# A gated attention block with mixture of experts: another order of the engines' steps in each pass over two sequences, the experts' rows cut at 352 in place of 384, and the third output tile placed on either side of the branch

## The chip, the cores and the metric

One Trainium2 chip, one core. The metric is the device time of one execution in microseconds (us), as the median of several runs. TensorE (PE) multiplies, VectorE (DVE), ScalarE (ACT) and GpSimd (POOL) work elementwise, SyncE (SP) issues most of the transfers. Each engine runs its own instruction stream in order; semaphores join the streams.

## The reference

Sixteen sequences `x` of 128 tokens and 256 features are normalized and attend to a context in a sliding window (two batches of 1024 tokens, 16 heads of 16, blocks of 128). The result, times `tanh(g_xattn)`, is added to `x`. Then a mixture of 8 experts follows, with the two best experts for each token and room for 640 rows per expert:

```
xn = layernorm(x) * gamma + beta;  probs = softmax(xn @ Wr.T);  two best experts per token
rank = place of the (token, expert) pair among its expert's; kept if rank < 640
buf[expert, rank] = xn[token]
g, u = buf @ W12.T (halves of 2048);  h = silu(g) * u;  y = h @ W3.T
x = x + tanh(g_ffn) * sum over kept pairs of prob * y[expert, rank]
```

Run through the reference, these inputs send 225, 328, 984, 337, 706, 204, 671 and 641 rows to experts 0 to 7, so that experts 0, 1, 3 and 5 have at most 337 rows and the other four fill all 640.

## The kernel before

**Attention and routing.** Eight passes (`body`, n = 0 to 7), each over two sequences in eight steps g (one per group of four heads). Every engine has its own `body`, with the order in a step written out by hand; semaphore counts hold the streams together. A group's work goes from engine to engine: PE `scores` into one of two PSUM banks, DVE `largest` (L941), ACT `exps` (L631), two steps later PE `prob_columns` (transposes, L1317), ACT `high_probs` (L638) and DVE `low_probs` (L946, which splits the probabilities into two halves), another step later PE `weigh_values` (L1331). `scores` of step g waits for `exps` of step g-2. Between these, each pass carries the keys, queries and values of the next two sequences (PE L1251, L1241, L1258; ACT `keys`, `queries`, `values`, `values1`, `values2`; DVE `keys_low` L978 and `queries_low` L985; POOL `values_rest`, `values_third`, `normalize_inputs`), the output of the two before (DVE `heads_out` and `heads_scale`; PE `output_columns` L1339, ACT `output_columns` L624, PE `project_out` L1345, DVE `gated` L973, which needs POOL's `residual` L428) and the routing of the two before those (`clip_logits` to `slots`; `pslot` is L930, `gate_columns` L901). `ranks` and `slots` use the PSUM bank `Xo`, and so do the logits and the output columns. Finished rows are scattered into `expert_rows` by POOL's indirect transfers.

**Experts.** Eight experts in turn. Weights and rows are split into a high and a low half in float32r, so that each product is three matmuls (`three`, L1485 to L1487). An expert's rows go through `up` in two chunks, 384 and 256 wide; the second chunk is taken only where `more_rows` says that the expert has more rows than the first holds. `up` has 8 steps of 12 matmuls with the chunk as moving columns; `down` makes an output tile of 128 rows from 24 matmuls with 256 moving columns. The order on PE is up(chunk 0), rows of the next expert, tiles 0 and 1, rows of the next expert, tile 2, and then, in the branch, up(chunk 1), tiles 3 and 4. ACT (`steps`) takes silu and rounds, DVE multiplies, takes the low halves and weighs the tiles (`weigh` L1181), and splits the next expert's weights meanwhile. POOL adds each tile to the output by an indirect transfer.

Of the kernel before, what the change touches and what calls it, by code (L numbers as in the profile page):

```python
# [15 lines left out]
P = 128  # L16
# [14 lines left out]
CHUNKS = ((0, 384), (384, 256))  # L31
FT = FF // P
CT0 = CHUNKS[0][1] // P
# [13 lines left out]
def gated_block(nc, x, ctxT, gates, biases, wqT, wkT, wvT, woT, bo, gamma, beta, wrT, w12T, w3T, out):  # L47
    with ExitStack() as top:
# [83 lines left out]
        slot = sb(pa, "slot", [P, SB, E], F32)  # L132
# [19 lines left out]
        hH = [sb(pc, f"hH{c}", [P, FT, w], F32R) for c, (_, w) in enumerate(CHUNKS)]  # L152
        hL = [sb(pc, f"hL{c}", [P, FT, w], F32R) for c, (_, w) in enumerate(CHUNKS)]
# [45 lines left out]
        pe_out, dve_ysc = sem("pe_out"), sem("dve_ysc")  # L199
        added, added2, expert_added = sem("added"), sem("added2"), sem("expert_added")  # L200
# [24 lines left out]
        def _(sp):  # L225
# [102 lines left out]

            for (o, w), done in zip(CHUNKS, (ld_rows[0], ld_rows_rest)):
# [23 lines left out]
        def _(pool):  # L353
# [152 lines left out]
            body(0, 0, False, False, True, True, True, None)  # L506
# [6 lines left out]
            residual(0, 0, False)  # L513
            body(1, 1, True, False, True, True, True, None)
# [22 lines left out]
            pool.memset(lnv[:, :], 1.0).then_inc(pool_sent, 1)  # L537

# [34 lines left out]
        def _(act):  # L573
# [66 lines left out]
            def body(n, par, prev1, prev2, cur, nxt):  # L640
                for g in range(NG):
                    G = NG * n + g
                    if g == 7 and nxt:
                        values(n + 1, Xp)
                        values1(n + 1, 1 - par)
                    if (cur and g >= 2) or (prev1 and g < 2):
                        high_probs(G - 2, g % 2, not prev1 and g < 4)
                    if g == 0 and prev1:
                        output_columns(SB * (n - 1), Xo)
                    elif g == 2 and prev2:  # L650
                        x2_columns(n - 2, Xo)
# [8 lines left out]
                    if g in (1, 2) and cur and not prev1:  # L660
                        zero_low_keys(2 * g - 1)
                        if g == 1:
                            zero_low_keys(2)
                    elif g == 4 and prev2:
                        exps_of_logits(n - 2)
                    if g == 4 and prev1:
                        output_columns(SB * (n - 1) + 1, Xo)
                    if g == 4 and nxt:
                        queries(n + 1, 1 - par, Xp)

# [15 lines left out]
            for a in (2, 3):  # L686
                r = slice(a * HD, (a + 1) * HD)
                act.dma_start(kM[0][r, :, a:H:HR, :].bitcast(F32), k2[r, :, :, :].bitcast(F32)).then_inc(ld_km[0], 16)
            act.wait_ge(bias_ok, 1)
            queries(0, 0, Q0)  # L690
            values(0, Xo)
            values1(0, 0)
            body(0, 0, False, False, True, True)
# [35 lines left out]
            def rows_high(e, par, a):  # L729

                c, d = a // 2, a % 2
                o, w = CHUNKS[c]
                act.wait_ge(pe_bT, 4 * e + a + 1)
                act.activation(bXh[par][:, d, o:o + w], Xc[a % 2][:, 0:w], ACT.Copy).then_inc(act_bh, 1)

            def hidden_high(e, j):

                c, f = j // FT, j % FT
                w = CHUNKS[c][1]
                act.wait_ge(dve_h, 16 * e + j + 1)  # L740
                act.activation(hH[c][:, f, :], hF[j % 2][:, 0:w], ACT.Copy).then_inc(act_hh, 1)  # L741
# [63 lines left out]
        def _(dve):  # L805
# [114 lines left out]
            def slots(m, mpar, bank, one=None, probs_between=False):  # L920
# [7 lines left out]
                dve.scalar_tensor_tensor(slot[:, a:b, :], late[:, a:b, :], LATE, rk, ALU.mult, ALU.add).then_inc(dve_rk, 1)  # L928
                dve.wait_ge(dve_rk, R_SLOT * s + 2)
                dve.tensor_tensor(pslot[:, :, a:b, :], pick[:, :, a:b, :], slot[:, a:b, :].unsqueeze(1).to_broadcast([P, K, b - a, E]), ALU.mult)\  # L930
# [58 lines left out]
            def body(half, par, prev1, prev2, prev3, cur, nxt):  # L989
                n = 2 * half + par  # L990
                HPS = 2 * SB
                for g in range(NG):
                    G = NG * n + g
                    routed = n - 2 if prev2 else None
                    if g in (2, 6) and prev1:
                        gated(n - 1, 1 - par, g // 4, Xo)
                    if g == 4 and prev2:
                        clip_logits(routed, Xo)
                    elif g == 6 and prev2:
                        sort_experts(routed)  # L1000
                    if cur:
                        largest(G, g)
                    if g == 3 and nxt:
                        keys_low(n + 1, Xp)
                    elif g == 5 and nxt:
                        queries_low(n + 1, 1 - par, Xp)
                    if g == 5 and prev2:
                        sum_exps(routed)
                    if g == 4 and prev2:
                        sort_logits(routed)  # L1010
                    elif g == 5 and prev2:
                        guard_sum(routed)
                    if g == 4 and prev2:
                        shift_logits(routed)
                    elif g == 5 and prev2:
                        invert_sum(routed)
                    elif g == 6 and prev2:
                        pick_experts(routed)
                    if g in (4, 6) and cur and not prev1:
                        stats1(*XCUT[g // 2:g // 2 + 2])  # L1020
# [8 lines left out]
                    if (cur and g >= 2) or (prev1 and g < 2):  # L1029
                        low_probs(G - 2, g % 2)  # L1030
                    if g == 6 and prev2:
                        members(routed)
                        gate_columns(routed, par)
# [13 lines left out]
            zero_keys(1, 0, 0)  # L1047
# [86 lines left out]
            def rows_low(e, par, a):  # L1134
                c, d = a // 2, a % 2
                o, w = CHUNKS[c]
# [13 lines left out]
            def steps(i, par, c, last, first):  # L1150
                e = 2 * i + par
                w = CHUNKS[c][1]
                for f in range(FT + 1):
# [7 lines left out]
                    if f >= 1:  # L1161
                        jj = j - 1
                        dve.wait_ge(act_hh, 16 * e + jj + 1)
                        dve.tensor_tensor(hL[c][:, f - 1, :], hF[jj % 2][:, 0:w], hH[c][:, f - 1, :].bitcast(F32), ALU.subtract)\  # L1164
                           .then_inc(dve_hl, 1)
# [10 lines left out]
            def weigh(e, par, t, first):  # L1176

                if t == 0 and not (isinstance(e, int) and e < 2):
                    dve.wait_ge(expert_added, e - 1)
                dve.wait_ge(pe_out, CT * e + t + 1)  # L1180
                dve.tensor_scalar(ysc[par][:, t, :], Yb[(par + t) % 2][:, 0:D], rows[par][:, t, bass.ds(D + e, 1)], None, ALU.mult)\  # L1181
                   .then_inc(dve_ysc, 1)

            def expert(i, par, last, first):
# [15 lines left out]
                weigh(e, par, 2, first)  # L1200
# [4 lines left out]
                with dve.Else():  # L1205

# [15 lines left out]
        def _(pe):  # L1222
# [125 lines left out]
            def body(n, par, prev1, prev2, prev3, cur, nxt, use):  # L1348

                for g in range(NG):  # L1350
                    G = NG * n + g
                    if cur:
                        scores(G, g, n, par, not prev1 and g < 2)
                    if (cur and g >= 2) or (prev1 and g < 2):
# [13 lines left out]
                    if g == 1 and prev1:  # L1368
                        project_out(SB * (n - 1), Xo)
                    elif g == 2 and prev2:  # L1370
# [18 lines left out]
                    if g == 0 and prev1:  # L1389
                        if prev3:  # L1390
                            pe.wait_ge(dve_rk, R_SLOT * (n - 3) + 2)
                        elif prev2:
                            pe.wait_ge(dve_x2, SB * (n - 1))
                        else:
                            pe.wait_ge(dve_bo, 1)
                        output_columns(SB * (n - 1), Xo)
# [48 lines left out]
            pe.wait_ge(dve_rk, R_SLOT * (NSB - 3) + 2)  # L1445
# [22 lines left out]
            def rows_columns(e, par, use, a):  # L1468
# [4 lines left out]
                o, w = CHUNKS[c]  # L1473
# [47 lines left out]
            def down(e, par, c, t, parts):  # L1521

                o = t * P - CHUNKS[c][0]
                for f in parts:
                    if t in (0, CT0):
                        pe.wait_ge(dve_hl, 16 * e + FT * c + f + 1)
                    ins = three(Yb[(par + t) % 2][:, 0:D],
                                ((hH[c][:, f, o:o + P], hL[c][:, f, o:o + P]),
# [8 lines left out]
            def expert(i, par, last, first):  # L1537
# [16 lines left out]
                output_bank(e, 2, first)  # L1554
                down(e, par, 0, 2, range(FT))
                with pe.If(more_rows(flags, e)):
                    up(i, par, 1, first)
                    for t in range(CT0, CT):
# [41 lines left out]
```

## Time and profile before

| what | value |
|---|---|
| median of 3 runs | 530.26 us (529.48 to 530.85) |
| profiled execution, its own time | 527.21 us |
| span of the profiled execution | 525.3 us |
| mean granted TensorE clock | 0.967 |
| busy: PE, DVE, ACT, POOL | 480.7, 352.1, 295.5, 189.1 us |
| attention passes, roughly | 16 to 198 us |
| last routing, transfers, first rows | 198 to 231 us |
| experts on PE, then the last additions | 231 to 514, to 525.3 us |

The span runs from the first to the last instruction of that execution. Busy times come from one profiled execution, and the engines work side by side, so their sum says nothing; what sets the end is read stage by stage.

### The profile page before, as it was taken

To read this page: it belongs to the slowest core of one execution; us is meant where nothing else is said; L and a number is where in the kernel's file an instruction comes from. 1 tells how busy PE (TensorE), PEld (TensorE's weight loads), DVE (VectorE), ACT (ScalarE), POOL (GpSimd) and SP (SyncE) were. 2 spreads that over 40 slices of the span, in tenths; PEclk is the share of its full clock that TensorE was granted. 3 is DMA by queue.
4 is the path that set the end of the run, shared out by engine and by line. 5 is a ranking of instruction groups with operands and counts; after the bars stand their busy time and mean duration, and the time that the engine had idled before them with its cause. 6 is when DMAs were issued, how large, how long until landed. Compare 5 with 4: busy or idle time off the path is not lost.

```text
span 525.3 us, 10673 instructions
## 1 busy us (share of the span) xinstructions
PE 480.7 (92%) x3566; PEld 443.5 (84%) x3588; DVE 352.1 (67%) x864; ACT 295.5 (56%) x747; POOL 189.1 (36%) x257
## 2 busy tenths in 40 slices
PE   4887999999999997489999999999999999999991
PEld 3666887878878775389899999999999999999991
DVE  5495879797798998658776764585834867534340
ACT  5776777777877773427564643464632737324130
POOL 8406573857768476600203020203032030310302
PEclk9999999999999997589999999999999999999997
DMA  5979413414142611273666551355541474200111
GB/s 163 255 177 283 81 19 63 83 52 91 56 90 55 210 51 48 71 225 125 193 211 181 145 175 17 73 186 138 175 95 22 130 191 133 31 11 11 16 15 20
DMA packets 41650, 57.34 MB, mean 109 GB/s; under 512 B 3721, under 2 KB 38576, under 8 KB 39552
## 3 DMA queue, kind: packets, MB, share of 16 engines
q1 hardware_dynamic: 35008, 48.49, 31.4%
q0 software_dynamic: 6144, 8.07, 9.1%
q8 instruction: 28, 0.46, 0.4%
q10 hardware_dynamic: 448, 0.14, 0.2%
q14 instruction: 22, 0.18, 0.1%
HBM read 36.24 MB, written 16.72 MB: 101 GB/s over the span
## 4 chain that ended last, share of the span: by engine, by line
PE 55%; DVE 2%; issue 2%; POOL 1%; DMA 1%; ACT 0%; POOLq 0%; DVEq 0%
PE bank L1485 18%; PE bank L1487 17%; PE bank L1486 17%; PE bank L1479 2%; DMA expert_rows<-xr,slotu 1%; PE bank L1413 1%; PE bank L1279 0%; POOL expert_rows L475 0%; POOL out_tokens L547 0%; PE bank L1271 0%; DVE pT L946 0%; DVE xr L842 0%; DVE xr L840 0%; DVE ysc L1181 0%; ACT xnT L585 0%
## 5 line engine op out<-in xcount | busy, mean ns | idle before, releaser
L547 POOL DMA_INDIRECT out_tokens<-ysc,rows x32 | 49.4, 1544 | 243.7 <-DVE ysc L1181 236.5
L1485 PE MATMUL bank<-bXh,wh 128*128 128x384 f32 (+1 forms) x384 | 122.0, 318 | 1.5 <-issue 1.2
L1487 PE MATMUL bank<-bXh,wl 128*128 128x384 f32 (+1 forms) x384 | 121.8, 317 | 0.0
L1486 PE MATMUL bank<-bXl,wh 128*128 128x384 f32 (+1 forms) x384 | 121.8, 317 | 0.0
L761 ACT ACTIVATE sil<-bank 128x384 f32<-128x384 f32 (+1 forms) x96 | 43.7, 456 | 126.6 <-PE bank L1487 126.5
L1160 DVE TENSOR_TENSOR hF<-sil,bank 128x384 f32<-128x384 f32 (+1 forms) x96 | 48.9, 509 | 76.1 <-ACT sil L761 76.1
L631 ACT ACTIVATE p<-bank,nm 128x128 f32<-128x128 f32 x256 | 73.5, 383 | 30.9 <-DVE nm L941 30.9
L1485 PE MATMUL bank<-wh,hH 128*128 128x256 f32 x256 | 73.8, 288 | 0.3 <-DVE ysc L1181 0.3
L1486 PEld LDWEIGHTS bank<-bXl,wh 128*128 128x128 f32 x384 | 72.7, 189 | 1.4 <-issue 1.4
L1485 PEld LDWEIGHTS bank<-bXh,wh 128*128 128x128 f32 x384 | 72.7, 189 | 0.5 <-issue 0.5
L1487 PEld LDWEIGHTS bank<-bXh,wl 128*128 128x128 f32 x384 | 72.6, 189 | 0.0
L1487 PE MATMUL bank<-wh,hL 128*128 128x256 f32 x256 | 72.4, 283 | 0.0
L1486 PE MATMUL bank<-wl,hH 128*128 128x256 f32 x256 | 72.4, 283 | 0.0
L1307 PE MATMUL bank<-kM,q 128*128 128x512 f32 x192 | 67.8, 461 | 0.1
L1131 DVE TENSOR_TENSOR wl<-stage,wh 128x512 fp32r<-128x512 f32 x96 | 63.1, 684 | 3.3 <-ACT wh L726 1.8
L726 ACT ACTIVATE wh<-stage 128x512 fp32r<-128x512 f32 x96 | 56.7, 622 | 1.6 <-DMA stage<-in_w3T 1.6
L1485 PEld LDWEIGHTS bank<-wh,hH 128*128 128x128 f32 x256 | 49.0, 191 | 1.3 <-DVE ysc L1181 0.7
L941 DVE TENSOR_REDUCE nm<-bank 128x4 f32<-128x512 f32 x64 | 43.5, 679 | 8.6 <-PE bank L1307 8.4
L1164 DVE TENSOR_TENSOR hL<-hF,hH 128x384 fp32r<-128x384 f32 (+1 forms) x96 | 48.7, 507 | 0.7 <-ACT hH L741 0.5
L1486 PEld LDWEIGHTS bank<-wl,hH 128*128 128x128 f32 x256 | 49.1, 192 | 0.0
L1487 PEld LDWEIGHTS bank<-wh,hL 128*128 128x128 f32 x256 | 49.0, 191 | 0.0
L946 DVE SCALAR_TENSOR_TENSOR pT<-bank,pT 128x512 f16<-128x512 f32 x64 | 43.6, 682 | 6.1 <-ACT pT L638 6.0
(144 smaller groups left out, 821.8 us busy)
## 6 DMA issues: line engine op xcount, KB each, us to landing
stage<-in_w12T SPq DMA_DIRECT2D x16, 1024.0 KB, 4.8
stage<-in_w3T SPq DMA_DIRECT2D x8, 1024.0 KB, 5.6
expert_rows<-padrow SPq DMA_DIRECT2D x8, 662.5 KB, 8.5
rows<-expert_rows SPq DMA_DIRECT2D x7, 662.5 KB, 4.3
kM<-k SPq DMA_DIRECT2D x62, 64.0 KB, 2.4
cT<-in_ctxT SPq DMA_DIRECT2D x8, 256.0 KB, 3.3
out_tokens<-x_all SPq DMA_DIRECT2D x8, 256.0 KB, 2.3
x_all<-in_x SPq DMA_DIRECT2D x2, 640.0 KB, 5.8
```

The lines of the kernel that those rows point to most:

```text
L547: pool.indirect_dma_start(out=out, out_offset=bass.IndirectOffsetOnAxis(rows[par][:, c, D + E:ROW].bitcast(U32), 0), in_=ysc[par][:, c, :] ...
L631: ins = act.activation(p32[g % 2][:, h, :], S[g % 2][:, h * T:(h + 1) * T], ACT.Exp, bias=nm[g % 2][:, h:h + 1])
L726: act.activation(Wh[par][:, k, q * QW:(q + 1) * QW], stage[s][:, q * QW:(q + 1) * QW], ACT.Copy)\
L761: act.activation(sil[j % 2][:, 0:w], Gb[j % 2][:, 0:w], ACT.Silu).then_inc(act_sil, 1)
L946: dve.scalar_tensor_tensor(pT[g % 2][:, 1, :, :], Tb[g % 2][:, :].rearrange("p (h t) -> p h t", h=GH), PSCALE, pT[g % 2][:, 0, :, :], ALU. ...
L1131: dve.tensor_tensor(Wl[par][:, k, cols], stage[s][:, cols], Wh[par][:, k, cols].bitcast(F32), ALU.subtract)\
L1160: dve.tensor_tensor(hF[j % 2][:, 0:w], sil[j % 2][:, 0:w], Ub[j % 2][:, 0:w], ALU.mult).then_inc(dve_h, 1)
L1164: dve.tensor_tensor(hL[c][:, f - 1, :], hF[jj % 2][:, 0:w], hH[c][:, f - 1, :].bitcast(F32), ALU.subtract)\
L1307: ins = nc.tensor.matmul(S[g % 2][:, :], q2[par][:, sq, hq // 2, b * T:(b + 1) * T], kM[par][:, sk, GH * hq:GH * hq + GH, b * T:(b + 1) * ...
L1485: nc.tensor.matmul(out_ap, ah, bh, start=start, stop=False)
L1486: nc.tensor.matmul(out_ap, ah, bl, start=False, stop=False)
L1487: return nc.tensor.matmul(out_ap, al, bh, start=False, stop=stop)
```

## The change

- **The chunks** are 352 and 288 rows wide (`CHUNKS`); the rows' transposes and their splitting keep the old 384 and 256 (`TILED`). `hH` and `hL` become one tile each over all 640 columns.
- **The third output tile** (`SPLIT` = 2) leaves the common part. Where the second chunk is taken, it comes after `up` of that chunk, with tiles 3 and 4. Elsewhere it is made in a new `Else` from the 96 rows (`REST`) that chunk 0 has left. POOL clears the unused 32 rows of that tile once (`spare_ok`).
- **DVE:** in each step `low_probs` goes ahead of `heads_out` (in step 0 ahead of `largest`); `keys_low` goes ahead of `largest`; `guard_sum` and `invert_sum` go to step 6, `gate_columns` to the end of step 7, behind `slots`. `slot` is a part of the PSUM bank `Xo` and no longer a tile in SBUF. One `zero_keys` goes from before pass 0 into its step 1.
- **ACT:** `values` of the next pass goes behind `high_probs` of step 7, `values1` from step 7 to step 0 of the next pass, `values2` from step 0 to step 1, `output_columns` from step 0 to the start of step 1, `keys` from step 3 to the end of step 2, `x2_columns` behind `exps`; the three `zero_low_keys` of pass 0 go ahead of it.
- **PE:** `output_columns` goes from the end of step 0 to step 1 (behind `scores`), and waits for `slots` one count longer; `project_out` goes to the end of step 1.
- **POOL:** `values_third(1)` goes from pass 0 to behind `residual(0)`.

```diff
-CHUNKS = ((0, 384), (384, 256))
+CHUNKS = ((0, 352), (352, 288))
+TILED = ((0, 384), (384, 256))
+SPLIT = 2
+REST = CHUNKS[0][1] - SPLIT * P
...
 # POOL
-            body(0, 0, False, False, True, True, True, None)
+            normalize_inputs(2)
+            values_rest(1, 1)
...
             residual(0, 0, False)
+            values_third(1, 1)
...
+            pool.memset(ysc[0][REST:P, SPLIT, :], 0.0).then_inc(spare_ok, 1)
...
 # ACT, body
-                    if g == 7 and nxt:
-                        values(n + 1, Xp)
-                        values1(n + 1, 1 - par)
+                    if g == 1 and prev1:
+                        output_columns(SB * (n - 1), Xo)
                     if (cur and g >= 2) or (prev1 and g < 2):
                         high_probs(G - 2, g % 2, not prev1 and g < 4)
                     if g == 0 and prev1:
-                        output_columns(SB * (n - 1), Xo)
-                    elif g == 2 and prev2:
-                        x2_columns(n - 2, Xo)
-                    elif g == 3 and nxt:
-                        keys(n + 1, Xp)
+                        values1(n, par)
+                    elif g == 7 and nxt:
+                        values(n + 1, Xp)
                     if cur:
                         exps(G, g, not prev1 and g < 2)
-                    if g == 0 and cur:
+                    if g == 0 and cur and not prev1:
                         values2(n, par)
                     if g == 0 and nxt:
                         input_columns(n + 1)
...
+                    elif g == 1 and prev1:
+                        values2(n, par)
+                    elif g == 2 and nxt:
+                        keys(n + 1, Xp)
+                    if g == 2 and prev2:
+                        x2_columns(n - 2, Xo)
...
 # DVE, slots and body
-                dve.scalar_tensor_tensor(slot[:, a:b, :], late[:, a:b, :], LATE, rk, ALU.mult, ALU.add).then_inc(dve_rk, 1)
+                slot = bank[:, 2 * SB * E:2 * SB * E + (b - a) * E].rearrange("p (j e) -> p j e", e=E)
+                dve.scalar_tensor_tensor(slot, late[:, a:b, :], LATE, rk, ALU.mult, ALU.add).then_inc(dve_rk, 1)
...
+                    if g == 0 and prev1:
+                        low_probs(G - 2, g % 2)
+                    if cur:
+                        largest(G, g)
...
+                    if (cur and g >= 2) or (prev1 and g == 1):
+                        low_probs(G - 2, g % 2)
...
                     if g == 7 and prev2:
                         slots(routed, par, Xo)
+                        gate_columns(routed, par)
...
 # PE, body and expert
+                    if g == 1 and prev1:
+                        if prev3:
+                            pe.wait_ge(dve_rk, R_SLOT * (n - 3) + 3)
...
+                        output_columns(SB * (n - 1), Xo)
                     if (cur and g >= 2) or (prev1 and g < 2):
                         prob_columns(G - 2, g % 2, not prev1 and g < 4)
...
-                    if g == 0 and prev1:
...
-                        output_columns(SB * (n - 1), Xo)
+                    if g == 1 and prev1:
+                        project_out(SB * (n - 1), Xo)
...
-                output_bank(e, 2, first)
-                down(e, par, 0, 2, range(FT))
                 with pe.If(more_rows(flags, e)):
                     up(i, par, 1, first)
-                    for t in range(CT0, CT):
+                    for t in range(SPLIT, CT):
                         output_bank(e, t, first)
                         down(e, par, 1, t, range(FT))
+                with pe.Else():
+                    output_bank(e, SPLIT, first)
+                    down(e, par, 0, SPLIT, range(FT), REST)
```

## Rows read from the trace of the kernel before

**Rows 1.** Busy time by stretch; us, busy per engine (instructions), PE clock, DMA share, GB/s

```profile
106.00:129.00 23.00, 22.25 (x181) 18.48 (x183) 19.36 (x57) 17.69 (x52) 16.55 (x22) 1.00 0.31 71
```

**Rows 2.** Waits of PE: releaser, us in total, times, longest

```profile
PE bank L1331 <- DVE pT L946: 7.2, 10, 2.7
...
PE bank L1485 <- issue: 1.2, 1, 1.2
...
PE bank L1485 <- DVE ysc L1181: 0.3, 1, 0.3
```

**Rows 3.** PE in passes 0 and 1; brackets: idle before, releaser

```profile
27.76 1.97 PE L1241 MATMUL bank<-xT,wq 128*128 128x256 f32 x8 [1.63 <-DVE k L978]
...
50.25 0.46 PE L1331 MATMUL bank<-V,pT 128*128 128x50 bf16 x8 [2.73 <-DVE pT L946]
...
53.27 2.13 PE L1241 MATMUL bank<-xT,wq 128*128 128x256 f32 x8
```

**Rows 4.** Experts on PE: start us, us, line, operands, count

```profile
283.84 0.28 PE L1486 MATMUL bank<-wl,hH 128*128 128x256 f32 x1
...
286.24 0.34 PE L1485 MATMUL bank<-bXh,wh 128*128 128x384 f32 x1
...
288.32 0.33 PE L1485 MATMUL bank<-bXh,wh 128*128 128x384 f32 x1
```

**Rows 5.** ACT in pass 0

```profile
20.97 2.06 ACT L672 ACTIVATE kM<-ident 128x1024 fp32r<-128x1024 f32 x2
```

**Rows 6.** DVE in pass 1

```profile
48.43 0.48 DVE L973 SCALAR_TENSOR_TENSOR x_all<-bank,tg,xbo 128x256 f32<-128x256 f32 x1 [4.28 <-POOL xbo L428]
```

**Rows 7.** POOL in pass 1

```profile
42.53 1.16 POOL L422 TENSOR_TENSOR V<-vf,V 128x512 bf16<-128x512 f32 x1 [4.05 <-ACT V L619]
...
47.02 2.54 POOL L428 TENSOR_TENSOR xbo<-x_all,tbo 128x512 f32<-128x512 f32 x2
```

**Rows 8.** One stretch of that time: us, PE busy, PE clock, DMA share, GB/s

```profile
51.00:52.00 1.00, 1.00 (x3) 0.50 0.58 191
```

**Rows 9.** PE from step 0 of pass 5 to step 0 of pass 6

```profile
131.90 0.38 PE L1304 MATMUL bank<-causal,identb 128*128 128x512 bf16 x1
...
136.28 1.03 PE L1345 MATMUL bank<-wo,oT 128*128 128x256 f32 x4
...
137.47 1.05 PE L1307 MATMUL bank<-kM,q 128*128 128x512 f32 x3
...
147.32 0.38 PE L1304 MATMUL bank<-causal,identb 128*128 128x512 bf16 x1
...
155.04 0.38 PE L1304 MATMUL bank<-causal,identb 128*128 128x512 bf16 x1
```

**Rows 10.** DVE in the same pass

```profile
134.65 0.74 DVE L930 TENSOR_TENSOR pslot<-pick,slot 128x32 f32<-128x32 f32 x1
...
135.52 0.68 DVE L941 TENSOR_REDUCE nm<-bank 128x4 f32<-128x512 f32 x1
...
144.07 0.88 DVE L978 SCALAR_TENSOR_TENSOR k<-bank,bqkv,k 128x256 fp32r<-128x256 f32 x2 [1.10 <-ACT k L604]
...
148.43 0.69 DVE L941 TENSOR_REDUCE nm<-bank 128x4 f32<-128x512 f32 x1 [0.27 <-PE bank L1307]
...
149.52 0.88 DVE L985 SCALAR_TENSOR_TENSOR q<-bank,bq,q 128x256 fp32r<-128x256 f32 x2 [0.39 <-ACT q L595]
```

**Rows 11.** ACT in the same pass

```profile
135.14 0.38 ACT L624 ACTIVATE oT<-bank 128x256 f32<-128x256 f32 x1 [0.24 <-PE bank L1339]
...
136.24 1.14 ACT L631 ACTIVATE p<-bank,nm 128x128 f32<-128x128 f32 x4 [0.71 <-DVE nm L941]
...
137.83 0.58 ACT L590 ACTIVATE xT<-bank 128x512 f32<-128x512 f32 x1
```

**Rows 12.** Line L930 over the run: count, ns min/median/max, first and last start

```profile
L930 DVE TENSOR_TENSOR pslot<-pick,slot x9: 174/728/739, 88.0 to 219.8; 128x32 f32<-128x32 f32 x7, 128x16 f32<-128x16 f32 x2
```

**Rows 13.** POOL beside that line in pass 5

```profile
134.61 0.73 POOL L460 TENSOR_TENSOR xr<-xr,gab 128x256 f32<-128x256 f32 x1
```

More of the change, by code:

```diff
@@ L151, in gated_block @@
         bXl = [sb(pc, f"bXl{i}", [P, DC, CAP], F32R) for i in range(2)]
-        hH = [sb(pc, f"hH{c}", [P, FT, w], F32R) for c, (_, w) in enumerate(CHUNKS)]
-        hL = [sb(pc, f"hL{c}", [P, FT, w], F32R) for c, (_, w) in enumerate(CHUNKS)]
+        hH = sb(pc, "hH", [P, FT, CAP], F32R)
+        hL = sb(pc, "hL", [P, FT, CAP], F32R)
         sil = [sb(pc, f"sil{i}", [P, 384], F32) for i in range(2)]
@@ L327, in _ @@
                 sp.wait_ge(scattered[s], 16 * K * SEQS // 2)
-            for (o, w), done in zip(CHUNKS, (ld_rows[0], ld_rows_rest)):
+            for (o, w), done in zip(TILED, (ld_rows[0], ld_rows_rest)):
                 if o > 0:
@@ L537, in _ @@
             pool.memset(lnv[:, :], 1.0).then_inc(pool_sent, 1)
+            for done in scattered:
+                pool.wait_ge(done, 16 * K * SEQS // 2)
+            pool.wait_ge(pool_sent, 1)
+            pool.memset(ysc[0][REST:P, SPLIT, :], 0.0).then_inc(spare_ok, 1)
+            pool.wait_ge(spare_ok, 1)
+            pool.memset(ysc[1][REST:P, SPLIT, :], 0.0).then_inc(spare_ok, 1)
+            pool.wait_ge(spare_ok, 2)
             pool.wait_ge(st_x2, 16 * NSB)
@@ L669, in body @@
                         queries(n + 1, 1 - par, Xp)
+                    if g == 4 and prev2:
+                        exps_of_logits(n - 2)
             def zero_low_keys(quarter):
@@ L996, in body @@
                         gated(n - 1, 1 - par, g // 4, Xo)
+                    if g == 3 and nxt:
+                        keys_low(n + 1, Xp)
                     if g == 4 and prev2:
                         clip_logits(routed, Xo)
+                    if g == 0 and prev1:
+                        low_probs(G - 2, g % 2)
+                    if cur:
+                        largest(G, g)
+                    if g == 4 and prev2:
+                        sort_logits(routed)
+                    elif g == 5 and nxt:
+                        queries_low(n + 1, 1 - par, Xp)
                     elif g == 6 and prev2:
                         sort_experts(routed)
[L1001 to L1012, printed above, removed]
+                    if g == 1 and cur and not prev1:
+                        zero_keys(1, 0, 0)
+                    if g in (4, 6) and cur and not prev1:
+                        stats1(*XCUT[g // 2:g // 2 + 2])
+                    if (cur and g >= 2) or (prev1 and g == 1):
+                        low_probs(G - 2, g % 2)
                     if g == 4 and prev2:
@@ L1015, in body @@
                     elif g == 5 and prev2:
-                        invert_sum(routed)
+                        sum_exps(routed)
                     elif g == 6 and prev2:
                         pick_experts(routed)
-                    if g in (4, 6) and cur and not prev1:
-                        stats1(*XCUT[g // 2:g // 2 + 2])
+                        guard_sum(routed)
+                        members(routed)
+                        invert_sum(routed)
                     if g in (1, 3) and prev1:
@@ L1028, in body @@
                         heads_scale(HPS * n + k, k, SB * n - 1 if prev1 else None)
[L1029 to L1033, printed above, removed]
                     if g in (2, 6) and prev1:
@@ L1174, in steps, with weigh @@
                         low(i + par, 1 - par, f)
-            def weigh(e, par, t, first):
+            def weigh(e, par, t, first, n=P):
                 if t == 0 and not (isinstance(e, int) and e < 2):
                     dve.wait_ge(expert_added, e - 1)
+                if t == SPLIT and isinstance(e, int) and e < 2:
+                    dve.wait_ge(spare_ok, e + 1)
                 dve.wait_ge(pe_out, CT * e + t + 1)
-                dve.tensor_scalar(ysc[par][:, t, :], Yb[(par + t) % 2][:, 0:D], rows[par][:, t, bass.ds(D + e, 1)], None, ALU.mult)\
+                dve.tensor_scalar(ysc[par][0:n, t, :], Yb[(par + t) % 2][0:n, 0:D], rows[par][0:n, t, bass.ds(D + e, 1)], None, ALU.mult)\
                    .then_inc(dve_ysc, 1)
@@ L1366, in body @@
                             values(n + 1, 1 - par, Xp)
-                    if g == 1 and prev1:
-                        project_out(SB * (n - 1), Xo)
-                    elif g == 2 and prev2:
+                    if g == 2 and prev2:
                         pe.wait_ge(dve_x2, SB * (n - 1) + 1)
```

56 lines of the change are left out of this document (25 added, 31 removed).

## Prediction

> **What bounds the kernel now.** I read the table by stretch first, then PE's waits, then PE's own timeline, and the other engines only where PE stands still. In the middle of the attention part PE is busy 22.25 of 23.00 us, at full clock, while DVE is busy 19.36, ACT 17.69 and POOL 16.55 [rows 1]: PE sets the pace there, and DVE has little to spare. The waits of PE [rows 2] name three things that this change touches: 7.2 us for `low_probs` in ten places, 1.2 us of "issue" and 0.3 us for a weighed tile, the last two in the experts. Up to the last expert PE hardly stands still there, so the expert part is a count of columns. The early passes hold the longest waits, 1.63 and 2.73 us [rows 3].
>
> The profiled execution took 527.21 us, of which 525.3 are the span; the median of the runs is 530.26, 3.05 us more. My terms are differences on the profiled one, and I carry their sum to the median.
>
> **Experts: the chunks.** Twenty matmuls with 256 moving columns take 283.84 to 286.24, that is 0.120 us each, and twelve with 384 take 286.24 to 288.32, 0.1733 each [rows 4]. On the line through both a column costs 0.417 ns, so 352 columns take 0.160 and 288 take 0.1333 us. A chunk has 96 matmuls. An expert without the second chunk saves 96 x 0.0133 = 1.28 us; experts 0, 1, 3 and 5 are such, and since none has 353 to 384 rows, no expert changes its branch: -5.12. An expert with both chunks pays 96 x (0.160 + 0.1333) = 28.16 us, as much as 96 x (0.1733 + 0.120): nothing. Tile 2 keeps 24 matmuls of 256 moving columns, whether 96 or 128 rows come out, so I count nothing; no row has 96 output rows, and between nothing and 24 x 0.120 = 2.9 us per tile in either direction I take the row with the same moving columns. In the other four experts tile 2 moves behind `up` of chunk 1, which needs no result of tile 0; the 0.3 us that the last expert waits for a weighed tile [rows 2] go: -0.3. Engines off PE are covered: a step of `up` still takes 12 x 0.160 = 1.92 us on PE, and DVE's two passes over fewer columns get shorter too. POOL clears the spare rows long before its first addition, so that costs nothing.
>
> The new `Else` puts a jump close ahead of PE's work, behind 12 matmuls in place of a whole tile. No row shows a jump by itself; the nearest is the 1.2 us of "issue", once in the run [rows 2]. Per expert without the second chunk the price lies between nothing and that; four times it would be 4.9. I take half of one, +0.6. Experts in all: -5.12 - 0.3 + 0.6 = -4.8 us.
>
> **Passes 0 and 1.** In pass 0 the queries' matmuls wait 1.63 us for `keys_low` [rows 3]. Two things ahead of that go: 2.06 us of zeroing on ACT [rows 5], now before the pass, and one `largest` (0.68 us [rows 10], about 0.6 from start to start) on DVE. That is more than PE stood still there; with a shorter wait one step earlier (about 0.6) I count -2.4. DVE gets one `zero_keys` in its step 1, hidden by ACT's own work.
>
> In pass 1 DVE's `gated` waits 4.28 us for `residual` [rows 6], `low_probs` is queued behind it, and PE stands still 2.73 us [rows 3]. On POOL, `residual` is late because `values_third` waited 4.05 us for ACT before it [rows 7]. Now `residual` goes first. What POOL waits for instead is ACT's `values1`, now in step 0 of pass 1: a step later, but still before 42.53. From it `values_rest`, the variances, the gate and `residual` are some 6 us without a wait, which ends near 44 instead of at 47.02 plus half of 2.54, 48.3; and PE needs it only near 45. The whole 2.73 go. Behind that wait PE's clock was at half [rows 8]: the 3.02 us from 50.25 to 53.27 [rows 3] are about 1.5 at full clock. So -1.5 as well.
>
> **The steady passes.** Here a step is lost, and this is the main term against the change. Call the start of `scores` of step 5 zero. Before, step 0 of the next pass starts at 155.04 - 147.32 = 7.72, and step 2 another 137.47 - 131.90 = 5.57 later: 13.29 [rows 9]. ACT's `exps` of step 0 waits for DVE [rows 11]: DVE starts step 5 at 148.43 and, nearly without a gap, reaches `largest` of the next step 0 at 135.52 plus the period, 23.14: 10.23 us later [rows 10]. So `exps` starts at 136.24 + 23.14 - 147.32 = 12.06.
>
> On DVE the chain becomes 0.39 shorter, as `queries_low` need not wait for ACT behind another copy [rows 10]; 0.55 shorter, as `pslot` takes 0.18 and not 0.73 [rows 12]; and, by my estimate, 0.2 shorter, as `guard_sum` and `invert_sum` no longer stand directly behind what they wait for. It becomes 0.6 longer, as `low_probs`, which runs over the same 512 columns as `largest`, now stands ahead of it in step 0, and I add 0.15 for a wait for `high_probs` in step 7. `exps` of step 0 starts near 11.7.
>
> The price of `pslot` rests on rows: it took 728 ns at the median and 174 at the least [rows 12], and in pass 5 it ended at 135.39, just behind POOL's product of 134.61 to 135.34 [rows 10, 13]. The Trainium skill (SBUF, "Who interferes with whom") says that a VectorE instruction with two SBUF inputs contends with a GpSimd instruction that reads SBUF, and one with at most one SBUF input outside the 2-port modes does not; by that rule, with which these rows agree, `slot` in PSUM frees `pslot`.
>
> But `project_out` is now behind this chain. ACT copies the output columns in step 1, behind `exps` and `input_columns` of step 0. So `project_out` starts at 11.7 + 1.14 (`exps`) + 0.58 (`input_columns`) + 0.38 (`oT`) [rows 11], less 0.1 by which these overlap: 13.7. PE would be ready near 11.3, two steps of `scores` and transposes after 7.72; it takes 0.87 of the 1.19 us between 136.28 and 137.47 [rows 9], and step 2 starts at 14.55. That is +1.25 against 13.29. The `low_probs` stall of step 0, which the new order does remove, is already inside this difference. From step 2 to step 5 PE gains about 0.25, because the queries' matmuls wait for `keys_low`, which ended at 144.95 [rows 10] and now comes two steps' work earlier. Net +1.0 per pass.
>
> Added up: passes 0 and 1 give -2.4 - 2.73 - 1.5, and +1.6 for the same new wait between them: -5.0. From pass 1 to 2 there are no `slots` on DVE, but PE had next to no wait to lose: +1.9 - 0.25. Passes 2 to 6: 4 x 1.0; into pass 7, which has no `input_columns`, +0.8; inside pass 7 about -0.5 of waits for `gated`. Attention: +1.0 us. Each of the five steady terms is good to 0.4, so -1 to +3.
>
> **PE's clock** is a term by itself. The new wait lasts about 2.4 us in every pass, between transposes and a few short matmuls. Before, the clock fell to its lower level of 1.2 GHz behind 2.73 us of standing still with transposes ahead of it [rows 3], and did not behind the 1.63. The new one lies between them. A fall costs 1.5 us by the same rows. Over six passes I count one: +1.5, between nothing and 9.
>
> Sum: -4.8 + 1.0 + 1.5 = -2.3 us; the profiled span would be 523.0, and the median **528.0 us**.
>
> **Rivals.**
> - *The clock falls behind most of the new waits* (slower). Place: step 1 of each pass, behind `project_out`. Six falls are 9 us in place of 1.5: 535.5; it decides from four falls on (-2.3 + 4.5 is +2.2). For it: the wait repeats and has only transposes and `weigh_values` around it. Against: it is shorter than 2.73. Chance 0.17, at 532 to 536.
> - *The new wait costs nothing*, because DVE's chain shortens by more than I found or PE's queue holds enough work. Then the passes add nothing after pass 1, and the rest stays: -5.0 - 4.8 = -9.8, 520.5. For it: DVE stands still before step 5, so a shorter chain counts at once. Against: the order on ACT is fixed, and `exps` is ahead of `output_columns`. Chance 0.20.
> - *Every jump to `Else` is paid*: 4 x 1.2 in place of 0.6, 532.3. For it: one "issue" wait stood behind the first skipped branch. Against: three others showed none [rows 2]. The Trainium skill (Runtime: NRT & Kernel Launch, "Instruction fetch mechanics") says that a taken branch out of the fetched window forces a fetch before execution goes on; no run here shows the window, and by that rule the 1.2 could come four times. Chance 0.09.
> - *`gate_columns` waits for POOL.* It reads two SBUF inputs, and now comes behind `slots`, when POOL is in the middle of its products of 0.73 us [rows 13]. If it waits as long as `pslot` did, 0.55 us come back in each of five passes: +2.8, 530.8, no change. The Trainium skill (SBUF, "Who interferes with whom") speaks for it. Chance 0.11.
> - My forecast, 525.5 to 530: 0.43.
>
> **How the numbers follow.** A measurement of this kernel can't tell 0.3% (1.6 us) from no change. Faster by more holds in most of the forecast (0.35 of 0.43) and in the second rival: 0.55. Within 0.3%: 0.07 of the forecast, most of the third and fourth rival: 0.24. Slower: the first rival and the rest of the third: 0.21. The range for 8 in 10 reaches from a little under the second rival, 519.5, into the first, 533.5. The forecast's own is 525.5 to 530.
>
> **What would show it.** Matmuls with 352 columns every 0.160 us, and experts without the second chunk 1.28 us shorter. No 2.73 us wait in pass 1, and `residual` ending near 44. `pslot` at 0.18 us. A wait for ACT's `oT` ahead of `project_out` in step 1 of passes 2 to 7, near 2.4 us, and a period of 24.1 instead of 23.14. Stretches at the lower clock before 198 us. If that wait isn't there, the sum is wrong by 5 us or more; if the columns don't cost what the line says, by up to 5 in the other direction.

## Result and the profile after

| | before | after |
|---|---|---|
| median of runs, us | 530.56 (529.48 to 531.73, 4 runs) | 538.69 (535.39 to 540.32, 4 runs) |
| profiled execution, us | 527.21, span 525.3 | 538.1, span 536.4 |
| first matmul of the experts, us | 231.03 | 235.82 |
| from there to the end of the last matmul, us | 282.9 | 289.3 |

The changed kernel is slower: 1.016 times the time of before (95% interval 1.0132 to 1.0189). I had forecast 528.0, and 519.5 to 533.5 as the range.

PE's waits in the changed kernel answer to [rows 2]: releaser, us in total, times, longest. ("issue" is idle time for which the profile shows nothing that the engine waited for.)

```profile
PE bank L1362 <- ACT oT L636: 13.4, 8, 2.1
PE bank L1502 <- issue: 9.9, 2, 5.4
...
PE bank L1348 <- DVE pT L961: 0.8, 2, 0.4
```

The first line is the wait that the change was forecast to add, for `oT` ahead of `project_out`. The third is what is left of the 7.2 us for `low_probs`. The second line is new in its size: 9.9 us in two places, where before had 1.2 us in one. L1502 is `three`, the experts' matmul. Here are the two places on PE, and between them two matmuls of expert 1 that show the new columns (start us, us, operands; in brackets the idle time before and its releaser):

```profile
258.96 0.36 PE L1502 MATMUL bank<-wh,hH 128*96 128x256 f32 x1
...
259.86 0.28 PE L1503 MATMUL bank<-wl,hH 128*96 128x256 f32 x1
259.98 0.28 PE L1504 MATMUL bank<-wh,hL 128*96 128x256 f32 x1
264.65 0.37 PE L1502 MATMUL bank<-wh,hH 128*96 128x256 f32 x1 [4.40 <-issue]
264.82 0.41 PE L1503 MATMUL bank<-wl,hH 128*96 128x256 f32 x1
265.04 0.41 PE L1504 MATMUL bank<-wh,hL 128*96 128x256 f32 x1
...
275.83 0.32 PE L1504 MATMUL bank<-bXh,wl 128*128 128x352 f32 x1
275.99 0.32 PE L1502 MATMUL bank<-bXh,wh 128*128 128x352 f32 x1
...
358.43 0.60 PE L1496 MATMUL bank<-ident,rows 128*128 128x128 f32 x4
364.48 0.52 PE L1502 MATMUL bank<-wh,hH 128*96 128x256 f32 x1 [5.45 <-issue]
```

Both stalls stand in the `Else` that the change adds (only there are 96 rows put out): in expert 0 after nine of its 24 matmuls, in expert 3 before the first. Experts 1 and 5 run the same code with no stall. After both, the matmuls step by 0.21 us and no longer by 0.12; the table by stretch shows why (us, busy us per engine, then PE's granted clock, DMA share, GB/s):

```profile
90.00:94.00 4.00, 4.00 (x14) 3.17 (x13) 2.95 (x8) 2.44 (x9) 3.52 (x4) 0.57 0.22 72
264.70:267.70 3.00, 3.00 (x15) 3.00 (x15) 0.00 (x0) 0.00 (x0) 0.00 (x0) 0.50 0.91 230
364.40:370.40 6.00, 5.92 (x27) 5.93 (x28) 0.35 (x1) 0.00 (x0) 0.00 (x0) 0.51 0.07 11
```

The clock is at its lower level, 1.2 GHz, for about 3 and 6 us behind the two stalls, and once in attention, in pass 3. While expert 3 stands still, the DMA queues move this (kind: packets, MB, share of 16 engines); first the stretch from 358.3 to 361.8 us, whole, then from 361.9 to 363.1:

```profile
q1 hardware_dynamic: 174, 1.20, 85.5%
```

```profile
q0 software_dynamic: 130, 0.12, 82.7%
q8 instruction: 1, 0.02, 4.9%
q1 hardware_dynamic: 1, 0.00, 0.0%
```

q1 carries the weights, in loads of 1 MB, and q8 brings 16 KB of PE's code at a time. The jump is on record at 358.35 us and lasts 5.97; the fetch of code starts at 361.99, when the load of weights has ended, and takes 0.95; PE's sequencer goes on at 364.32.

### The profile page after: what moved, and what is told of

It is laid out like the page before. It is cut to its first block, busy times and chain, and to the rows that moved or that the text cites. A ratio compares the mean times of both kernels' runs of the same rounds, so it can differ in the third digit from the quotient of the medians.

```text
span 536.4 us, 10682 instructions
## 1 busy us (share of the span) xinstructions
PE 478.3 (89%) x3566; PEld 444.0 (83%) x3588; DVE 347.9 (65%) x864; ACT 295.4 (55%) x747; POOL 189.6 (35%) x259
## 4 chain that ended last, share of the span: by engine, by line
PE 53%; issue 3%; DVE 2%; POOL 1%; DMA 0%; another core or an unknown queue 0%; DVEq 0%; ACT 0%; POOLq 0%
PE bank L1502 17%; PE bank L1503 17%; PE bank L1504 17%; PE bank L1496 2%; PE bank L1430 1%; POOL expert_rows L478 1%; DMA expert_rows<-xr,slotu 0%; POOL out_tokens L559 0%; DVE osum L970 0%; DVE ysc L1198 0%; DVE x_all L988 0%; DVE st L841 0%; DVE pT L961 0%; DVE bXl L1153 0%
## 5 line engine op out<-in xcount | busy, mean ns | idle before, releaser
L1502 PE MATMUL bank<-bXh,wh 128*128 128x352 f32 (+1 forms) x384 | 121.0, 315 | 0.3 <-DVE bXl L1153 0.3
L1503 PE MATMUL bank<-bXl,wh 128*128 128x352 f32 (+1 forms) x384 | 120.5, 314 | 0.0
L1504 PE MATMUL bank<-bXh,wl 128*128 128x352 f32 (+1 forms) x384 | 120.4, 313 | 0.0
L1175 DVE TENSOR_TENSOR hF<-sil,bank 128x352 f32<-128x352 f32 (+1 forms) x96 | 47.9, 499 | 70.6 <-ACT sil L775 66.5
L1502 PE MATMUL bank<-wh,hH 128*128 128x256 f32 (+1 forms) x256 | 74.9, 293 | 10.0 <-issue 9.9
L1503 PE MATMUL bank<-wl,hH 128*128 128x256 f32 (+1 forms) x256 | 74.0, 289 | 0.0
L1504 PE MATMUL bank<-wh,hL 128*128 128x256 f32 (+1 forms) x256 | 74.0, 289 | 0.0
L1502 PEld LDWEIGHTS bank<-bXh,wh 128*128 128x128 f32 x384 | 72.4, 189 | 0.5 <-issue 0.5
L1502 PEld LDWEIGHTS bank<-wh,hH 128*128 128x128 f32 (+1 forms) x256 | 49.4, 193 | 6.2 <-issue 5.7
L1503 PEld LDWEIGHTS bank<-wl,hH 128*128 128x128 f32 (+1 forms) x256 | 49.6, 194 | 4.5 <-issue 4.5
L1504 PEld LDWEIGHTS bank<-wh,hL 128*128 128x128 f32 (+1 forms) x256 | 49.6, 194 | 0.0
```

The lines of the kernel that those rows point to most:

```text
L1175: dve.tensor_tensor(hF[j % 2][:, 0:w], sil[j % 2][:, 0:w], Ub[j % 2][:, 0:w], ALU.mult).then_inc(dve_h, 1)
L1502: nc.tensor.matmul(out_ap, ah, bh, start=start, stop=False)
L1503: nc.tensor.matmul(out_ap, ah, bl, start=False, stop=False)
L1504: return nc.tensor.matmul(out_ap, al, bh, start=False, stop=stop)
```

## Theories

**Theory B**, the count of blocks. In straight code the fetches on q8 stand 260 recorded PE instructions apart (twelve from 27.7 to 206.6 us). The Trainium skill (Runtime: NRT & Kernel Launch, "Instruction fetch mechanics") gives blocks of 256 instructions, which agrees. A matmul counts two, since its weight load is one of its own. The `If` body is 339 instructions in the changed kernel (168 matmuls and 3 more) and 291 before (144 and 3). Nine matmuls and ten weight loads of expert 0's `Else` ran before the stall, so a border of blocks lies 19 instructions into it; from there the places of all jumps follow by counting. If PE asks for one block ahead, a jump is free where its target lies in the next block with enough code left in it:

| jump | starts, into its block | lands at | left to the border | stall, us |
|---|---|---|---|---|
| before, expert 0 | 201 | 493 | 19 | 1.2 |
| before, expert 1 | 86 | 378 | 134 | none |
| before, expert 3 | 155 | 458 | 54 and the loop's start | none |
| after, expert 0 | 153 | 493 | 19 | 4.4 |
| after, expert 1 | 87 | 427 | 85 | none |
| after, expert 3 | 254 | 606 | beyond the next block (512) | 5.45 |

Expert 5's jump is in the loop's second turn. From 374 to 447 us no code is fetched at all, so the loop's code was still there.

The rivals: that attention is what got slower (A), that each such jump has its price wherever it lies (L; the expectation of x3_flip calls its form of this "rival B"), and that the fetch is slow by itself, not behind the weights (F). In the first expectations theory B is still called J, without the count.

## Experiments

**Each half of the change alone.**

```
x1_experts:   before + CHUNKS ((0, 352), (352, 288)), SPLIT, Else on PE
x2_attention: before + the new order of the passes, slot in PSUM
```

> The kernel before with the experts' part of the change alone (chunks of 352 and 288, tile 2 on either side of the branch); attention as before. Theory J (the jumps to Else are what made the change slow): PE again stands still on issue for 4 to 6 us in two of the four experts without a second chunk, the clock falls behind it, and the time is 530.6 + 6 = 536 to 538. Rival A (the new order in the attention part is what made it slow, the experts gain their 4.8): 526.

> The kernel before with the attention part of the change alone; experts with chunks of 384 and 256 and no Else on PE. By the marks of the two traces the first matmul of the experts comes 4.8 us later, of which 1.1 at the start and 1.3 after the last pass: theory J expects 533 to 536, with no issue wait above 1.3 us. Rival A: 538 or more.

Measured: x1_experts 536.39 us (1.0101 of before, 1.0054 to 1.0149), x2_attention 531.67 (1.0022, 1.0000 to 1.0044); before, run beside them, 530.36. PE's waits on issue in the experts, first x1_experts, then x2_attention:

```profile
PE bank L1498 <- issue: 10.4, 2, 5.3
```

```profile
PE bank L1489 <- issue: 1.3, 1, 1.3
```

Rival A falls: the experts cost 6.0, attention 1.3 (0.0 to 2.3 by its interval). x2_attention is below its range, because I took 2.4 us of differences between two single executions for the change's own. In x1_experts the eight matmuls of the first queries take 3.75 us, although its code is that of before there, whose profiled execution had 1.97; here x1_experts, then before:

```profile
12.19 3.75 PE L1254 MATMUL bank<-xT,wq 128*128 128x256 f32 x8 [0.78 <-ACT xT L601]
```

```profile
11.73 1.97 PE L1241 MATMUL bank<-xT,wq 128*128 128x256 f32 x8 [0.78 <-ACT xT L590]
```

So the profiled execution of before, 3.05 us under its median, had a start that others of the same code don't have. The clock made it: these matmuls step by 0.22 us in before and by 0.43 in x1_experts, and the records of the clock, at its upper level, begin at 9.37 and 17.19 us. In each of the thirteen traces the matmuls step by 0.43 until that first record and by 0.22 from it on; for a stretch ahead of it a view prints 1.00 for want of a record.

**The branches of PE swapped.**

```
-                with pe.If(more_rows(flags, e)):
+                with pe.If(few_rows(flags, e)):     # tile 2, 96 rows
+                    ...
+                with pe.Else():                     # up of chunk 1, tiles 2 to 4
```

> The changed kernel with PE's two branches swapped: the short one (tile 2 of an expert without a second chunk, 48 PE instructions and their weight loads) falls through, and the experts with both chunks jump over it, a short way. Same work, same order of work. Theory J, with the distance of the jump as the cause: the 9.9 us of issue and both falls of the clock go, at most the 1.2 us that the kernel before had stays: 526 to 529. Rival B (each branch with work on both sides costs a stall, however far): four jumps of 4 us in the long experts, 538 or more.

Measured: 534.2 us (1.0057, 1.0031 to 1.0084), two stalls of 3.8 and 3.1 us (6.9 in all). Neither side had it: the long experts' short jumps cost nothing, against the rival, but the short experts must now jump over the long body behind their tile, and stall there. By theory B expert 0 lands at 542, beyond the next block. Expert 3 lands in the next one, but entered its own block only 48 instructions before the jump, so the next was, as I read it, asked for late. Distance alone is not it; place is.

**The weight loads cut.**

```
+CUT = UNIT // 16
...
+                        sp.dma_start(stage[s][:, 0:CUT], w12T[e, 0:P, 0:CUT]).then_inc(ld_st[s], 16)
```

> The changed kernel with the weight loads of experts 1 to 7 cut to 1/16 of their columns (left out: the other 15/16, so the weights used are stale); the branches as in the changed kernel. In the changed kernel the instruction fetch behind the two stalled jumps began 3.6 and 3.8 us after the jump, when the 1 MB load of weights had just ended. Theory Q (the fetch waits behind the weight load): fetches begin within 1 us of the jump, and the issue waits shrink from 9.9 us to 3 to 5; time 531 to 534. Rival F (the fetch itself takes that long): the issue waits stay at 9 to 10 us, 538.

Measured: 527.46 us, issue waits of 5.5 us:

```profile
263.68 0.27 PE L1502 MATMUL bank<-wh,hH 128*96 128x256 f32 x1 [2.33 <-issue]
263.79 0.28 PE L1503 MATMUL bank<-wl,hH 128*96 128x256 f32 x1
...
359.62 0.35 PE L1502 MATMUL bank<-wh,hH 128*96 128x256 f32 x1 [3.15 <-issue]
```

The fetches begin 1.13 and 1.03 us after the jumps, no longer 3.8 and 3.6. So 4.4 of the 9.9 us are the fetch waiting behind the weights, and 5.5 (a little more than I expected) its own time. The matmuls behind step by 0.11: the clock did not fall there, and the experts take 280.77 us in place of 289.35. That the median is some 4 us better than expected is explained only in part: this profiled execution took 530.68, since its clock fell at 88, 163 and 204 us, ahead of the experts, where the code is that of the changed kernel; the other runs took 525.99 to 532.62.

**PE's code moved, the work unchanged.**

```
+            for _ in range(350):                 # y1_aligned: 175 instructions; y2_shift: 190
+                pe.wait_ge(ident_ok, 1)
             pe.wait_ge(ld_wk, 16)
```

> The changed kernel, same work in the same order, with PE instructions added that only wait for something long done, so that the code behind them moves: 175 before the first matmul, 66 spread over up of expert 1, and 102 in the Else of the loop's first expert, which this input never runs. Theory B (fetched blocks): PE's code comes in blocks of 256 instructions, the next block is asked for when PE enters one, and a jump stalls where its target, or what follows it shortly, lies two blocks on, or where the block was entered just before the jump. By the count of instructions the three jumps that matter now start 72, 69 and 82 instructions into a block and end in the next one with at least 85 instructions left, or with the loop's start behind them: no issue wait above 1 us in the experts, no fall of the clock there, 538.7 - 9.9 - 3.5 = 525 to 527. Rival L (a taken jump over this much code costs its 4 to 5 us wherever it lies): the issue waits stay at 9 to 10 us, 538.

> The changed kernel with 190 such waiting instructions before PE's first matmul and nothing else. By theory B the jump of expert 0 now starts 87 instructions into a block and has 85 left behind its target: its stall goes. That of expert 1 starts 21 into a block, so that the next block is asked for too late: it now stalls, some 3 to 4 us. That of expert 3 ends two blocks on (188 + 352 is more than 512): it still stalls, 5 us. So two stalls, in experts 1 and 3 instead of 0 and 3, and 537 to 539. Rival L: the stalls stay in experts 0 and 3.

Measured: y1_aligned 540.91 us, y2_shift 550.34, both far over their ranges, since the added waits were not free: PE's first matmul comes 17.5 and 19.1 us later than in the changed kernel, 0.10 us per added instruction. What they were made for they show; first y1_aligned's waits on issue, then y2_shift's, then y2_shift's expert 3:

```profile
PE bank L1268 <- issue: 23.1, 1, 23.1
...
PE bank L1483 <- issue: 1.2, 1, 1.2
```

```profile
PE bank L1504 <- issue: 5.4, 2, 5.1
```

```profile
374.74 0.52 PE L1504 MATMUL bank<-wh,hH 128*96 128x256 f32 x1 [5.13 <-issue]
```

In y1_aligned 0.24 us are left in the experts, in expert 1 (L1483 is the count of rows ahead of them): from first to last matmul they take 276.55 us, not 289.35. In y2_shift expert 0's stall went and expert 3's stayed, as theory B has it; expert 1 waited 0.24 us, as in y1_aligned, and not 3 to 4. Its fetch started at 297.09, 3.0 us ahead of the jump and 0.5 behind the first packets of a load of weights, so it did not have to wait for that load's end. So the part of theory B about a block that is asked for late, read out of x3_flip after its result, missed here and is not shown. Rival L falls. The same with the 165 waits in a branch never taken:

```
+            never = pe.value_load(iota_i[0:1, 0, 0:1], min_val=0, max_val=1)
+            with pe.If(never > 0):
+                for _ in range(330):
+                    pe.wait_ge(ident_ok, 1)
```

> The changed kernel with its PE code moved as in y1_aligned, but at no time of its own: the 165 waiting instructions ahead of the first matmul stand in a branch that is never taken (its test and its jump pass while PE waits for the first weights). Jumps of experts 0, 1 and 3 start 67, 64 and 77 instructions into a block. Theory B: experts take 276.6 us from their first matmul to the last, as in y1_aligned, against 289.3 in the changed kernel, and 525 to 527 in all. Rival L: 538.

Measured: 523.3 us (0.9884, 0.9819 to 0.9949), below the range; experts 276.46 us. The profiled execution also has no fall of the clock in attention, where the changed kernel's lost 1.6 us. The changed kernel, its code moved by some hundred instructions, is 1.2% faster than before. The fetches show why: one comes at 250.35, ahead of the jump of expert 0 at 256.14, and the next only at 260.09, when that tile is done, so what the jump lands on was there. That the place of a jump in the blocks makes its stall is shown.

**The new wait of `project_out` taken back**, on top of x2_attention.

```
-                    if g == 1 and prev1:
+                    if g == 0 and prev1:
...
                         output_columns(SB * (n - 1), Xo)
```

> The kernel with the attention part of the change alone, but output_columns and project_out of step 0 and 1 back at their places of before (on PE and on ACT). My prediction priced the new wait of project_out for oT at +1.25 us in each of the passes 1 to 7, against about 0.25 gained elsewhere. By that the 13.4 us of waits for oT go, low_probs of step 0 stays ahead of largest, and the time is 531.7 - 7 x 1.25 - 1.6 for the fall of the clock = 521 to 523. Rival W (the wait only moves: with output_columns in step 0, PE waits there for the probabilities or for slots instead): 529 to 532.

Measured: 527.21 us (0.9953, 0.9929 to 0.9977). Between the two: steady passes take 23.52 us, 24.17 in x2_attention and 23.14 before, from one `project_out` to the next. The wait for `oT` is gone and the clock does not fall in pass 3 (it does in pass 1, at 49 us), but new waits come; PE's waits there:

```profile
PE bank L1283 <- ACT xnT L586: 4.4, 6, 0.8
...
PE bank L1343 <- DVE pslot L934: 3.2, 5, 0.9
```

So only about half of my 1.25 comes back (0.65 per pass, and 2.3 in pass 3, where the clock fell); the rest moves on, part of it to `slot` in PSUM, whose bank `output_columns` must wait for. Rival W has a share in it.

**The early passes, and all that is good together.**

```
y4_residual_first: POOL's order of pass 0 alone
z3_early_passes:   y4 + zeroing and keys_low of pass 0
z1_best:           z3 + experts of the change + the moved code
```

> The kernel before with nothing but POOL's order of pass 0: residual ahead of the values' third part. By the prediction's step the 2.73 us wait in pass 1 goes and with it the half clock, 1.5: 530.4 - 4.2 = 526. Rival (residual is still late, since values_rest of pass 1 waits for ACT in the same place): at most 1 us, 529.5 to 530.5.

> The kernel before with the order of pass 0 changed alone: POOL's residual first as in y4_residual_first, and the zeroing of keys and keys_low of pass 0 as in the change; every later pass as before. By the prediction's first two terms, as far as the traces bore them out (pass 0 from 21.8 to 19.2 us, pass 1 from 25.0 to 21.6): 530.0 - 2.6 - 3.4 = 524. Rival (the start gives back what pass 0 saves, since the zeroing now stands before the first scores): 526.

> What the runs so far say is good, put together: z3_early_passes with the experts' part of the change and PE's code moved as in z2_after_aligned; the steady passes of attention as in the kernel before. Expected: 524 - 6.4 = 517 to 519. If the gains are not independent (the clock falls at other places): 520 to 523.

Measured: 526.22 us (0.9924, 0.9895 to 0.9954), 522.55 (0.9865, 0.9804 to 0.9927) and 515.96 (0.9729, 0.9671 to 0.9786). Pass 1 takes 21.6 us in all three and 25.0 before, pass 0 takes 19.15 in the last two and 21.85 before. The gains add up, the last two come out over 1 us below their expectation, and z1_best beats both kernels.

## Why the prediction was wrong

**The step that failed** is the jump to `Else` in the experts' part: "I take half of one, +0.6", between nothing and 4 x 1.2 = 4.9. Measured: 12.8 us in all (289.35 against 276.55 us in y1_aligned). Of these 9.9 are stalls. The lower clock behind them cost 4.1: 15 matmuls at 0.21 in place of 0.12 us are 1.5, and from expert 3's jump to the next expert's it took 8.06 us longer than in y1_aligned, 5.45 of them the stall. Some 1.2 come off again in expert 1, where y1_aligned waits about 1.0 us around the transposes of rows (mostly for `bXl`) and the late PE does not. My bound was a remainder taken for a price. The 1.2 us of "issue" [rows 2] was already a fetch behind expert 0's jump: on record at 256.38 us, PE stood still only from 260.1 to 261.4:

```profile
259.80 0.33 PE L1487 MATMUL bank<-bXh,wl 128*128 128x384 f32 x1
261.37 0.33 PE L1485 MATMUL bank<-bXh,wh 128*128 128x384 f32 x1 [1.23 <-issue]
```

Jump to restart is 5.0 us, of which 3.7 were covered by matmuls already queued. In the changed kernel jump to restart is 6.1 (258.53 to 264.65) and the cover 1.7. The prediction saw the cover go ("behind 12 matmuls in place of a whole tile") and did not add it back to the bound: four times 5 is 20.

The rival with every jump paid had the mechanism, at a quarter of its size, and on the wrong count: two of four stalled. The sentence of the Trainium skill that stood beside it (Runtime: NRT & Kernel Launch, "Instruction fetch mechanics"), on a target outside the fetched window, is borne out for expert 3, whose target lies beyond the next block. In expert 0 the target was there: the stall came 19 instructions behind it, where its block ends.

**The rest, point by point.**

- Columns: 352 columns take 0.160 us (275.83 to 275.99), as worked out. Without stalls the experts gain 282.93 - 276.55 = 6.4. That it equals the 5.12 of my sum and the 1.2 of the fetch that before had is partly luck: the 0.3 for the weighed tile went too, and 1.2 were lost in expert 1. Tile 2 with 96 rows steps by 0.12 like 128: nothing, as I chose.
- Pass 0 was put at -2.4 and gave -2.7. Pass 1 was put at -4.2 (stall and half clock); POOL's order alone gave -3.4 by the passes and 3.5 us in the time (y4_residual_first). `residual` ended at 44.8, forecast "near 44":

```profile
43.51 1.30 POOL L431 TENSOR_TENSOR xbo<-x_all,tbo 128x512 f32<-128x512 f32 x1
```

- Steady passes: `exps` of step 0 came 11.66 us behind step 5, forecast 11.7; `project_out` 13.61, forecast 13.7; step 2 at 14.61, forecast 14.55; the period is 24.21, forecast 24.1. These rows answer to [rows 9, 11]; the first is step 5 ahead of `exps`:

```profile
149.64 0.38 PE L1321 MATMUL bank<-causal,identb 128*128 128x512 bf16 x1
```

```profile
161.30 1.14 ACT L643 ACTIVATE p<-bank,nm 128x128 f32<-128x128 f32 x4 [1.29 <-DVE nm L956]
...
162.80 0.41 ACT L636 ACTIVATE oT<-bank 128x256 f32<-128x256 f32 x1
```

One pass earlier, step 5 and what follows it:

```profile
125.48 0.38 PE L1321 MATMUL bank<-causal,identb 128*128 128x512 bf16 x1
...
139.09 1.13 PE L1362 MATMUL bank<-wo,oT 128*128 128x256 f32 x4 [2.08 <-ACT oT L636]
140.09 1.04 PE L1324 MATMUL bank<-kM,q 128*128 128x512 f32 x3
```

- `slot` in PSUM: `pslot` takes 186 ns at the median, forecast 0.18, and `gate_columns` did not take over the wait, so that rival falls. It agrees with what the Trainium skill (SBUF, "Who interferes with whom") says; no run tried `slot` alone.

```profile
L945 DVE TENSOR_TENSOR pslot<-pick,bank x9: 170/186/186, 85.4 to 223.5; 128x32 f32<-128x32 f32 x7, 128x16 f32<-128x16 f32 x2
```

- The clock: one fall in attention, +1.5 in the sum. It came in pass 3 (25.84 us against 24.21, 1.6). The rival of six falls did not come. But the one is no property of the kernel: with the same order and the same waits for `oT`, the clock fell nowhere in the passes of y1_aligned and z2_after_aligned, and in two of them in x4_small_loads. That the clock could fall in the experts was in no term.
- Attention and its clock were put at +2.5 and cost 1.3 (x2_attention). With 12.8 - 1.2 = 11.6 for the jumps in place of 0.6, my sum would have been 539.0; measured 538.69. So near a hit is partly luck, since the attention terms alone were 1.2 too high and the runs lie between 535.39 and 540.32.

## What to carry to other kernels

A short wait on "issue" behind a branch is what the queued work left uncovered: add the cover back before using it as a bound, and look for the fetch of code in the DMA view and for the loads that it has to wait behind. Where a branch is added or its body grows, count the instructions that it jumps over and where it lands: here the same work took 538.7 or 523.3 us by where the code lay. Before single executions are compared stage by stage, look at a stage whose code is the same in both, and at where the clock's records begin.

## What the hardware showed that I had not expected

- A fetch of 16 KB of code waits behind a load of weights: it started 3.6 and 3.8 us after the jump with 1 MB loads on their way, 1.0 and 1.1 with loads of a sixteenth.
- PE kept a whole loop's code, some 1,460 instructions: its second turn fetched none, although it jumps over 350 of them.
- A PE instruction that only waits for something long done costs 0.11 us when nothing covers it: in y1_aligned they stand 0.108 us apart from 4.12 to 22.78 us. That the first matmul came only 17.5 us later is because the wait for the first weights covered the first 1.2.
- PE's clock fell behind one of four equal waits of 2.08 us in attention, behind two of the same four in x4_small_loads and behind none in y1_aligned and z2_after_aligned; and in x4_small_loads not behind waits of 2.33 and 3.15 us among the experts' matmuls. What else decides stays open.
- Every trace starts at half speed: the first matmuls step by 0.43 us, and by 0.22 from the first record of the clock on. That record came ahead of the first queries in seven of the thirteen profiled executions, where their eight matmuls take 1.97 us, and during or behind them in six, where they take 3.41 to 3.75. What decides when it comes stays open.
